# A post-norm decoder layer on one core: engine programs in a hand-listed tile order, PSUM banks chosen per product

## What is computed

```python
x = layernorm(x + attn(x))
x = layernorm(x + xattn(x, ctx, ctx, mask))
x = layernorm(x + moe(x))
```

## Time and profile before

| | |
|---|---|
| median of three runs | 250.73 us |
| the profiled execution | 250.36 us |
| its span, first to last instruction | 248.6 us |
| PE busy | 221.0 us, 89% |
| DVE busy | 188.7 us, 76% |
| ACT busy | 174.7 us, 70% |
| POOL busy | 139.0 us, 56% |
| DMA, mean of 16 engines, over 10 to 20 us | 91%, 241 GB/s |

### The profile page before, as it was taken

How to read it: one execution, slowest core, us unless ns; L and a number is a source line. 1 busy time by engine, 2 the same in 40 slices (tenths; PEclk the granted TensorE clock), 3 DMA queues, 4 the chain that set the end, 5 groups by cost and what they waited for, 6 DMA issues and landing times.

```text
span 248.6 us, 7860 instructions
## 1 busy us (share of the span) xinstructions
PE 221.0 (89%) x2222; PEld 180.2 (73%) x2222; DVE 188.7 (76%) x696; ACT 174.7 (70%) x662; POOL 139.0 (56%) x367
## 2 busy tenths in 40 slices
PE   1867977999999999999999999999999999887740
PEld 1665866889898998878888878878887787664310
DVE  2265465665677678898898989898898988999864
ACT  4568978999967778786868778786866777653430
POOL 4446646644543627475755757575656556565542
PEclk9979999999999999999999999999999999999796
DMA  4793654544344242331433243342400000000000
GB/s 102 196 294 77 148 137 107 125 120 121 76 109 123 61 100 59 86 92 61 106 90 100 54 101 80 84 103 60 128 22 2 16 11 6 10 12 13 11 11 22
DMA packets 33706, 20.11 MB, mean 81 GB/s; under 512 B 20480, under 2 KB 31232, under 8 KB 33664
## 3 DMA queue, kind: packets, MB, share of 16 engines
q1 hardware_dynamic: 33232, 19.48, 30.8%
q10 hardware_dynamic: 432, 0.13, 0.2%
HBM read 14.16 MB, written 5.24 MB: 78 GB/s over the span
## 4 chain that ended last, share of the span: by engine, by line
PE 75%; DVE 8%; DMA 6%; SPq 4%; issue 3%; POOL 2%; ACT 1%; POOLq 0%; DVEq 0%; ACTq 0%
PE ps L690 12%; PE ps L758 9%; PE ps L657 7%; PE ps L577 6%; PE ps L705 6%; PE ps_probs L646 6%; PE ps_scores L626 6%; PE ps_probs L647 3%; PE ps_scores L628 3%; PE ps L606 3%; SPq L294 3%; PE ps L731 3%; DMA xbv_sb<-in_L_xattn_bv_dram 2%; PE ps L589 2%; DMA k_stack<-qk_scratch 2%
## 5 line engine op out<-in xcount | busy, mean ns | idle before, releaser
L1132 DVE TENSOR_REDUCE neg_max<-ps_scores 128x4 f32<-128x512 f32 x64 | 44.0, 687 | 18.4 <-PE ps_scores L628 18.2
L917 ACT ACTIVATE probs<-ps_probs 128x512 f32<-128x512 f32 x64 | 38.7, 605 | 2.7 <-PE ps_probs L647 2.5
L437 POOL TENSOR_SCALAR ms<-ss 128x1 f32<-128x1 f32 x48 | 11.1, 231 | 48.9 <-ACT junk L842 47.1
L758 PE MATMUL ps<-w_moe,y2T 128*128 128x512 f32 x64 | 34.3, 622 | 1.8 <-DVE z L1199 1.4
L690 PE MATMUL ps<-xT,guT 128*128 128x128 f32 x256 | 33.9, 275 | 0.4 <-ACT xT L941 0.4
L690 PEld LDWEIGHTS ps<-xT,guT 128*128 128x128 f32 x256 | 31.5, 191 | 1.0 <-ACT xT L941 0.8
L439 POOL TENSOR_TENSOR rs<-ms,neghalf 128x1 f32<-128x1 f32 x48 | 27.2, 567 | 4.0
L439 POOL TENSOR_TENSOR lrs<-ve,neghalf 128x1 f32<-128x1 f32 x48 | 26.4, 550 | 4.0
L626 PE MATMUL ps_scores<-k_stack,q_stack 125*128 125x128 bf16 x256 | 24.8, 219 | 1.6 <-DMA k_stack<-qk_scratch 1.2
L646 PE MATMUL ps_probs<-q_stack,k_stack 128*128 128x128 bf16 x256 | 24.7, 218 | 0.7 <-DMA q_stack<-nmT 0.7
L437 POOL TENSOR_SCALAR ve<-mv 128x1 f32<-128x1 f32 x48 | 9.2, 193 | 26.4 <-DVE mv L1209 11.0
(11 more groups left out here) (158 smaller groups left out, 617.3 us busy)
## 6 DMA issues: line engine op xcount, KB each, us to landing
q_stack<-qk_scratch SPq DMA_DIRECT2D x48, 96.0 KB
k_stack<-qk_scratch SPq DMA_DIRECT2D x48, 96.0 KB
qk_scratch<-qk_parts SPq DMA_DIRECT2D x16, 192.0 KB, 2.3
ctx_sb<-in_ctx_dram SPq DMA_DIRECT2D x4, 256.0 KB, 3.8
qk_scratch<-qk_parts SPq DMA_DIRECT2D x16, 64.0 KB, 2.2
out_dram<-x_all SPq DMA_DIRECT2D x16, 64.0 KB, 1.6
x_all<-in_x_dram SPq DMA_DIRECT2D x1, 640.0 KB, 8.6
raw<-in_L_ffn_Wi_dram SPq DMA_DIRECT2D x1, 512.0 KB, 7.0
```

What stands on the lines that cost most here:

```text
L758: nc.tensor.matmul(as_one(view(fill)), y2T[:, b, :], w_moe[:, 4 * n:4 * n + 4, :], start=True, stop=True).then_inc(S[("moe_m0_ps", "moe_m1 ...
L917: nc.scalar.activation(probs[:, n, :, :], ps_probs[:], ACT.Exp, scale=HD ** -0.5).then_inc(S["att_p"], 1)
L1132: nc.vector.tensor_reduce(neg_max[:, b, QUARTER * n:QUARTER * n + QUARTER], ps_scores[:], AX_X, ALU.max, negate=True).then_inc(S["max_max" ...
```

## The change

The pieces stay, and almost all their instructions. What changes:

- The functions `step`, `run`, `pair` and `once` go. Each engine's program is a flat list of calls with tile numbers (SP 70, POOL 194, PE 539, ACT 485 and DVE 510 calls). The tiles don't advance by one step each: the gru of ten tiles and the context of thirteen come ahead of the first turned scores, the other tiles' gru in the middle, and so on.
- The eight banks are one pool. A table `HOME` names the bank of each fill, a digit for each tile (for each quarter of the scores and turned scores too), and `bank_free` waits for the last reader of that bank, whatever it was.
- `att_values` is one burst of the 16 products of a tile behind all four exponentials; `probs` has two buffers for it.
- `moe_choose` has three calls: a memset over the places behind the best two, a match-replace and a comparison.
- The loads have a new order (the context's first quarter and the small projections earlier; the expert weights and both ffn weights all ahead of the first `parts_save`); Wqkv goes over ACT's queue. `parts_saved` has a semaphore for each buffer. The weights' transposes use any bank.
- Nine products of a zero tile run on PE ahead of the first transposes (`keep_busy`).
- Both masks on TensorE: the products with `above` and `below` are kept as they were.

The core of the diff:

```diff
+HOME = {
+    "gru_turn": "7702412544002713",
...
+    "scores": "6322065646254277774210275316654105712445125304343513242300263626",
+    "probs": "4625642644317413414341710136703507656360747631211747077415142517",
...
-        ps_scores = psum("ps_scores", [P, QUARTER, P])
-        ps_probs = psum("ps_probs", [P, QUARTER, P])
-        banks = [psum(f"ps_{n}", [P, 4, P]) for n in range(6)]
+        banks = [psum(f"ps_{n}", [P, 4, P]) for n in range(8)]
-        probs = sb("probs", [P, 4, QUARTER, P])
+        probs = sb("probs", [P, 2, 4, QUARTER, P])
...
-        def bank_free(eng, k, fill):
+        def bank_free(eng, fill, k):
-            bank = BANK[fill]
+            bank = HOME[fill][k]
             if bank in held:
                 after(eng, *held[bank])
             held[bank] = READER[fill], k + 1
...
+            def keep_busy(count):
+                for _ in range(count):
+                    nc.tensor.matmul(as_one(banks[4][:]), warm[:, 0:P], warm[:], start=True, stop=True)
+            pe.wait_ge(S["const_dve"], 1)
+            keep_busy(9)
...
-                after(pe, "max_max", 4 * k + n)
+                bank_free(pe, "scores", 4 * k + n)
...
-                after(pe, "att_p", 4 * k + n)
+                bank_free(pe, "probs", 4 * k + n)
...
+            def att_values(k):
+                b = k % 2
+                after(pe, "max_v", k + 1)
+                after(pe, "att_p", 4 * (k + 1))
+                bank_free(pe, "att_values", k)
+                for r in range(2):
+                    for t in range(2):
+                        for j in range(QUARTER):
+                            last = nc.tensor.matmul(view("att_values", k)[COLS * j:COLS * j + COLS, r, :],
+                                                    values[:, b, t, QUARTER * r + j, :], probs[:, b, 2 * r + t, j, :],
+                                                    start=(t == 0), stop=(t == 1))
+                last.then_inc(S["att_vT_ps"], 1)
...
+                nc.vector.memset(top[:, b, CHOSEN:EXPERTS], NO_LOGIT).then_inc(S["moe_pick"], 1)
+                after(dve, "moe_pick", 3 * k + 1)
+                nc.vector.match_replace(moe_new[:, b, :], top[:, b, :], moe_lg[:, b, :], -NO_LOGIT).then_inc(S["moe_pick"], 1)
+                after(dve, "moe_pick", 3 * k + 2)
+                nc.vector.tensor_tensor(moe_sel[:, b, :], moe_new[:, b, 0:EXPERTS], moe_lg[:, b, 0:EXPERTS], ALU.is_gt).then_inc(S["moe_pick"], 1)
```

The start of the loads on SP (after x, the gru weights and the columns), and stretches of the new lists:

```diff
+            load_x(1)
+            load_ctx(0)
+            load(raw_xk[:], xWk, "w_in_x")
+            load(raw_xq[:], xWq, "w_in_x")
+            load(raw[:, R_XWV, :], xWv, "w_in_o")
+            load(raw[:, R_WO, :], Wo, "w_in_o")
+            load_x(2)
...
+            load(raw[:, R_WI:R_WI + EXPERTS, :], Wi.rearrange("e d h -> d e h"), "w_in_e")
+            load(wmo_sb[:], Wmo.rearrange("e h d -> h e d"), "w_in_m")
+            load_small()
+            load_ctx(1)
+            load_out()
+            load_ctx(2)
+            parts_save(0)
+            load_ctx(3)
+            load_x(3)
+            parts_stack(0)
...
+            parts_stack(2)
+            max_stack(0)
...
+            parts_stack(6)
+            parts_save(7)
+            parts_stack(7)
+            max_stack(5)
+            max_stack(6)
+            parts_save(8)
+            parts_stack(8)
+            max_stack(7)
```

```diff
 PE:
+            qkv_turn(0)
+            ctx_project(2)
+            w_ei()
+            qk_project(0)
...
+            scores(6, 3)
+            moe_logits(1)
+            scores_turned(5, 2)
+            ffn_down(3)
+            scores_turned(5, 3)
+            moe_experts(1, 0)
+            ffn_turn(4)
+            max_turn(6)
+            att_values(5)
...
+            moe_turn(15)
+            moe_logits(15)
+            moe_experts(14, 1)
+            moe_experts(15, 0)
+            moe_experts(15, 1)
```

More of the change, by code:

```diff
@@ L517, in _, with turn_weights @@
+            moe_add(14)
+            moe_ln_power(13)
+            moe_add(15)
+            moe_ln_power(14)
+            moe_ln_power(15)
         @block.tensor
         def _(pe):
-            def turn_weights(home, first, count, done):
+            def turn_weights(fill, first, count):
+                bank_free(pe, fill, 0)
                 for n in range(count):
-                    last = nc.tensor.transpose(home[:, n, :], raw[:, first + n, :], ident[:])
-                last.then_inc(S[done], 1)
@@ L684, in ffn_hidden, with ffn_gate, ffn_up @@
+            def ffn_gate(k):
+                b = k % 2
                 if k == 0:
                     pe.wait_ge(S["w_gate"], 1)
+                ffn_hidden(k, "ffn_gate", 0, "ffn_gate_ps")
+            def ffn_up(k):
+                b = k % 2
+                if k == 0:
                     pe.wait_ge(S["w_up"], 1)
-                after(pe, "ffn_xT", k + 1)
-                bank_free(pe, k, fill)
-                for n in range(FF):
-                    last = nc.tensor.matmul(view(fill)[:, n, :], guT[:, g, n * P:(n + 1) * P], xT[:, 1, b, :], start=True, stop=True)
@@ L812, in _ @@
-            steps(step)
+                bank_free(pe, fill, k)
+                nc.tensor.matmul(as_one(view(fill, k)), y2T[:, b, :], w_moe[:, 4 * n:4 * n + 4, :], start=True, stop=True).then_inc(S[("moe_m0_ps", "moe_m1_ps")[n]], 1)
+            w_gru()
+            gru_turn(0)
+            gru_gates(0)
+            gru_turn(1)
+            w_qkv()
+            ctx_turn(0)
+            ctx_turn(1)
+            w_kq()
+            w_ox()
+            gru_turn(2)
+            gru_gates(1)
+            ctx_turn(2)
```

2832 lines of the change are left out of this document (2254 added, 578 removed).

## The result

The changed kernel takes 241.66 us, the median of four runs (240.00 to 243.57), beside 250.81 for the kernel before. The ratio is .9644, with a 95% interval of .9565 to .9722. The forecast was 234, faster, in a range of 222 to 249: the direction and the range held, and of the 16 us forecast 9 came.

What follows compares the result with a forecast made beforehand. The prediction took PE to bound the kernel's middle, with 201 us of work in a 248.6 us span; start 40 + middle 150.3 + end 42 = 232.3, plus 1.8 around it, gave 234 us, range 222 to 249.

Steps and rivals of the forecast that it cites:

- The start: Stretch until tile 0's turned scores: 40 us forecast (37.5 to 49.5), 42.3 before; turned scores 9.9 us after first scores.
- The middle: From tile 0's turned scores to tile 15's: 144.8 us of PE work x 1.038 = 150.3 us, 156.9 before.
- the 6 that it named as a sign of error: Sign for the middle: it is wrong if PE's waits there add up to more than 6 us.
- the 201 us of work: PE's products over the whole kernel, sixteen tiles and 5 us of weights, claimed to stay 201 us in the new order.
- The end: Stretch from tile 15's turned scores on: 28.7 + 3.9 + 8.9 = 41.5, taken as 42 us; 49.4 before.
- the 3.9 us for six hops of the last tile: At the end: tile 15 goes six times from a turn or product over a copy to the next product, .65 each.
- The tail: After PE's last product: sum, layer norm and store of one tile, claimed to stay at 8.9 us.
- The choice: DVE's choice of experts: 0 to .5 us less a tile, hidden in the middle; .4 on the path at tile 15.
- Half the gain: Rival: start at 44 and each tile .5 us late on the maxima's trip; 241 to 249 us, chance .14.
- the trip of the maxima: Middle, turn of the maxima to turned scores: 3.1 us unloaded, just covered by 3.25 us of other products on average.
- SP's queue: Rival: maxima's transfer 2.2 to 4.7 us late behind six copies at eight tiles; slower, 259 us, chance .14.
- The small edits at zero: Warm-up products at the start and both masks on TensorE were each put at 0 us.

Runs made afterwards that it cites:

- experiment 7: The kernel before with the new choice of experts (memset, match-replace, comparison) and nothing else; ratio .9949 to the kernel before, median 248.83 us.
- experiment 5: The changed kernel without the two mask products on TensorE; ratio .952 to the kernel before, median 239.23 us.
- experiment 11: The changed kernel with the mask product with `above` done twice in each quarter of scores; ratio .9816 to the kernel before, median 245.34 us.
- experiment 2: The changed kernel with the context's second load ahead of the three small loads in SP's list; ratio .9604 to the kernel before, median 241.17 us.
- experiment 3: The changed kernel with twelve unread products of the zero tile among the last tiles' products on PE; ratio .9624 to the kernel before.
- experiment 8: The changed kernel without the nine zero-tile products at the start; ratio .9622 to the kernel before, median 241.25 us.
- experiment 12: The changed kernel with the context's second load ahead of the small loads and twelve unread products near the end; ratio .9607 to the kernel before, median 241.04 us.
- experiment 10: The changed kernel without both mask products and with two of the four expert terms left out of DVE's mix; median 240.91 us, too uneven for a ratio.
- experiment 9: The changed kernel with tile 15's pieces moved ahead of those of earlier tiles at the lists' end, y2 three buffers; ratio .9739 to the kernel before, median 245.26 us.
- experiment 6: The changed kernel with the old five-operation choice of experts in place of the match-replace; ratio .9946 to the kernel before, median 251.22 us.
- experiment 4: The changed kernel with two of the four expert terms left out of DVE's mix; ratio .9689 to the kernel before, median 241.81 us.

## Why the prediction held in direction and missed by half

**The start.** "The turned scores come 9.9 us later, as now" is the term that failed: 13.5. Load order and the way to the first scores were right, q and k within .8 us and the scores inside their range; that the scores came there at 29.78 has some luck in it, since the same loads gave up to 33.6 in other profiles. I took the trip from a row of the old list, in which little that is foreign stands between a tile's last scores and its turned ones. In the new list tile 1's scores (.7 us), a cast on ACT that waits for a save (.9) and SP's copies for tile 2 (1.8) stand in it.

**The middle.** The figure was nearly right (150.3 against 151.7), the reason only half, so that the figure is near is partly luck. "PE bounds it, and no other engine would fill it" is true of the kernel before (the chain ran over PE alone, and experiment 7 shows DVE's savings worth nothing there). Of the new kernel it isn't: 15 us less for PE gave 2.8 (experiment 5), 8 us more cost 3.9 in the middle (experiment 11). By these two runs PE has some 4 us of slack, and what lies next to it is spread over copies, DVE, POOL and ACT. By the prediction's own measure 151.7 - 144.8 = 6.9 us were lost here, more than the 6 that it named as a sign of error; but the waits that show are for copies of a tile's parts, which none of its signs was. The prices of PE's products held (a quarter of scores .35, from 43.30 to 43.65; a pair of expert products .86, from 215.47 to 216.33), so the 201 us of work are not what was wrong. In the five profiles whose lists are the same through the middle (this one and those of experiments 2, 3, 8 and 12) it differed by up to 2.6 us (151.73 to 154.35), so these are sizes, not fine figures. Which of the others sets the 148 to 149 us that remained in experiments 5 and 10 is open.

**The end.** 42 was forecast, 45.5 measured. The step that failed is the way to PE's last product, and in it the 3.9 us for six hops of the last tile: 32.6 were forecast, 38.6 measured. The hops were waits of up to 1.36 us, and they were followed by the lower clock in the last products, which no term of mine held. The tail, "all of one tile, so this stays", was wrong too, 6.8 us and not 8.9, and hid a part of this. At full clock, in experiment 11, the two parts were 36.1 and 8.1. So the clock cost 1.2 to 1.5 us of the stretch, and some 2 us are left. That these are the last tile standing behind tiles 10 to 13 was my reading; experiment 9 speaks against mending it that way, and its cause stays open.

**The choice.** "Which DVE's 29 free us in the middle hide" is the largest error of reasoning. It didn't move the sum, which took the new lists together with the new choice, but it would have priced either without the other wrongly. The price per tile was right (.46 measured, 0 to .5 given; the old choice's 1.04 was read to the end of its last operation, start to start it is .98), the cover wasn't: in the new lists it is worth 7.6 us of the 9 (experiment 6), in the old ones 1.2 (experiment 7). I had written that 16 times the price "would count only were DVE the bound". DVE isn't busier than PE. In the changed kernel it has 3% of the chain in the middle, so work taken from it gives nothing there (experiment 4); with the old choice it has 15%, so the work added came out. My reading is that its list has no place left in which to be late.

**The rivals.** Half the gain is what came (241 to 249 were given, at .14), but by other causes: the trip of the maxima was covered at 15 tiles. SP's queue cost 1.8 us at one tile, far from the 2.0 on each of eight from which it would have decided. That SP's list also holds up copies behind the maxima's transfer, and that this is on the chain of the middle, the prediction didn't look at; what it costs no run shows. The small edits at zero (warm-up, both masks on TensorE) held.

## What to carry to other kernels

Where every engine runs a fixed list and the lists have been fitted to one another, a part's worth can't be read from one engine's free time: the same .46 us per tile was worth 1.2 us in lists that waited for PE alone and 7.6 in lists without slack. Here work added to such lists came out by a half (PE) to the whole (DVE), work taken away by a fifth or not at all; so undo each part in the new order before crediting the order with the gain. And before a transfer or a piece is moved up in one queue, follow what stands behind it: a wait taken from one tile came back larger at the next through two other queues.

## What the runs showed of the hardware

Issuing transfers back to back took SP .41 us each, now and then more (six copies from 37.66 to 40.30 with the maxima behind them, .44 on average), so the order of issue alone held up a small transfer by 1.82 us, where 2.57 to 3.00 pass from its issue to the product that reads it. A match-replace over 16 columns shows as two instructions of .09 and .16 us, and the whole choice took .48 us of DVE. With twelve products that nobody reads, put where PE waits, the last six expert products ran at full clock in both profiles, 2.82 us in place of 4.76; in the profiles of experiments 4, 10 and 11 they did so without them. Executions with the same start had a granted clock of 1.00 or of .67 to .86 from 20 to 30 us, and with the lower one tile 0's scores came at 31.3 to 33.6 us in place of 29.8 to 30.6.
